# Gathering routed tokens with four 32-row matmul tiles in fp32, and normalising on GpSimd

## Chip, core and metric

One core of one Trainium2 chip. The time is the device time of one execution in microseconds, the median of the runs shown. Engines are called PE (TensorE matmul), PEld (its weight loads), DVE (VectorE), ACT (ScalarE), POOL (GpSimd) and SP (SyncE).

## What is computed

A gated cross-attention block and a mixture-of-experts block, one after another, on x of 16 batches of 128 tokens with 256 features, all in fp32:

```python
x = x + tanh(g_xattn[0]) * xattn(layernorm(x), ctx, ctx, Wq, Wk, Wv, Wo, bo)
x = x + tanh(g_ffn[0]) * ffn(layernorm(x), controller, f1, bias, f2)
```

The attention has 16 heads of 16 features and a causal mask. In the feed-forward block the tokens of a batch form 4 groups of 32. Each of 128 slots (32 experts x 4 sets) takes, in each group, the one token with the largest logit:

```python
grouped = x.reshape(B, g, t, d)                      # g groups of t = 32 tokens, d = 256
logits = einsum('bgtd,des->bgtes', grouped, controller) + tie
perm = (logits == max(logits, axis=-3, keepdims=True))
dispatched = einsum('bgtd,bgtes->bgesd', grouped, perm)
inner = relu(einsum('bgesd,desf->bgesf', dispatched, f1) + bias)
intermediate = einsum('bgesf,esfd->bgesd', inner, f2)
out = einsum('bgesd,bgtes->bgtd', intermediate, perm)
```

The change concerns `dispatched`, the gather of the tokens by a permutation matrix of zeros and ones.

## The kernel before

The kernel has one program for each engine, with its order written out by hand and semaphores between them. It has four stages: loads and the first statistics (to some 13 us), attention batch by batch (to some 198 us, each batch in four chunks `c` of four heads), **routing** (to 231.6 us), the experts (to 295 us), and the combination with the store of the result. The change touches routing and the last attention batch, which already does the routing's first steps.

Routing works on one batch of 128 tokens at a time. For batch `b`:

- DVE normalises the rows: `xn[:, b % 4]`, 128x256 (`normalize`, L843). For batches 0 to 3 this is done within the last attention batch, for the others four batches ahead, and DVE waits for `rl_ready` of the slot's former batch.
- ACT rounds the rows to fp32r, `rh` (`rows_high`, L676), and POOL subtracts, `rl = xn - rh` (`split_rows`, L285). The slot of `xn` has then been read, except for the transposes.
- PE transposes the rows (`transpose_r`, L379) into bank 0, ACT keeps them as `rT` (`keep_r`, L664), PE makes the logits in bank 1 (`logits`, L384).
- DVE adds the tie ramp (`add_ramp`, L885, tile `lt`), takes the maximum of each group (L890) and compares (L895), which gives the permutation `pc` (slot x token), in two buffers. POOL copies it to `permT` (`keep_perm`, L290), which the last stage reads again.
- PE transposes `pc` (`spread`, L392) into bank 2 or 7. DVE multiplies it by a mask of groups into `permb` (`spread`, L901): token x (group, slot), 128x512, where the rows of other groups are zero.
- PE gathers (L528): for each half `h` of the features and each part (`rh`, `rl`) one full matmul of 512 columns, accumulated over the parts. The result of each half fills one bank. There are two sets of two banks (`BD`), used in turn.
- ACT moves both banks to `routed` (`keep_d`, L670), 2 x 512 columns. For the last two batches DVE moves one of the halves (L1031).

PE's order in the iteration for batch `b` is: logits of `b+2`, transposes of the rows of `b+3`, transpose of the permutation of `b+1`, gather of `b`. DVE's is: ramp of `b+2`, normalisation of `b+4`, maximum and comparison of `b+2`, masked copy of `b+1`. In the first four iterations DVE also runs the 13 stages of the inverse roots (`rstd`) of the last four batches. ACT's is: round rows of `b+3`, keep `rT` of `b+3`, move the gather of `b`. The first four and last four iterations are written out, the rest are loops of four.

When all of `routed` is kept, DVE gathers the experts' inputs into `xe` (L1038), and the expert stage begins. Its matmuls L548, as L348, L352, L368 in attention and L611 at the end, use tiles of 32 columns of the array.

Of the kernel before, what the change touches and what calls it, by code (L numbers as in the profile page):

```python
# [25 lines left out]
P = 128  # L26
# [23 lines left out]
def build(nc, x, ctxT, wattn, gbo, ctrl, wexp, constf, out):  # L50
    with ExitStack() as ctx:
# [6 lines left out]
        bank = [ctx.enter_context(nc.psum_tensor(f"bank{i}", [P, 512], F32)) for i in range(8)]  # L58
# [45 lines left out]
        rh = sb("rh", [P, 4, E], F32R)  # L104
        rl = sb("rl", [P, 4, E], F32R)
        lt = sb("lt", [P, P])
        gmax = sb("gmax", [P, NG])
        pc = sb("pc", [P, 2, P])
        permT = sb("permT", [P, NB, P])
        permb = sb("permb", [P, 2, NG, P], F32R)  # L110
# [57 lines left out]
        rh_ready = sem("rh_ready")  # L168
        rl_ready = sem("rl_ready")
# [7 lines left out]
        pm_ready = sem("pm_ready")  # L177
# [10 lines left out]
        permT_kept = sem("permT_kept")  # L188
# [48 lines left out]
        def _(pool):  # L237
# [44 lines left out]
            def split_rows(b, k4):  # L282

                pool.wait_ge(rh_ready, b + 1)
                pool.tensor_tensor(rl[:, k4], xn[:, k4], rh[:, k4].bitcast(F32), ALU.subtract).then_inc(rl_ready, 1)  # L285

            def keep_perm(b, k):

                pool.wait_ge(perm_ready, b + 1)
                pool.tensor_copy(permT[:, b, :], pc[:, k, :]).then_inc(permT_kept, 1)  # L290

            for b in range(3):
                split_rows(b, b)
            with pool.Fori(0, NB // 4 - 1) as i:
                b = i * 4
                for k4 in range(4):

                    keep_perm(b + k4, k4 % 2)
                    split_rows(b + (k4 + 3), (k4 + 3) % 4)
            for k4 in range(4):  # L300
                keep_perm(NB - 4 + k4, k4 % 2)
                if k4 < 1:
                    split_rows(NB - 1, 3)

            pool.wait_ge(permT_kept, NB)
# [11 lines left out]
        def _(pe):  # L317
# [56 lines left out]
            BR, BL, BP = bank[0], bank[1], (bank[2], bank[7])  # L374
            BD = ((bank[5], bank[6]), (bank[3], bank[4]))
# [128 lines left out]
            def route(b, k4, early=False, left=NB):  # L504

                k = k4 % 2
                if left > 2:
# [3 lines left out]
                if left > 3:  # L512
                    pe.wait_ge(rn_ready, b + 4)
                    transpose_r((k4 + 3) % 4)
                if left > 1:
                    if early and b == 0:

                        pe.wait_ge(x1_ready, NB)
                    spread(b + 1, 1 - k, first=early and b == 0)
# [12 lines left out]
            for b in range(4):  # L532
                route(b, b, early=(b < 2))
            with pe.Fori(1, (NB - 4) // 4) as i:
                b = i * 4
                for k4 in range(4):
                    route(b + k4, k4)
            for k4 in range(4):
                route(NB - 4 + k4, k4, left=4 - k4)
# [37 lines left out]
            pe.wait_ge(d_kept_dve, 2)  # L577
# [51 lines left out]
        def _(act):  # L629
# [37 lines left out]
            def keep_d(b, k, halves=KH):  # L667
                act.wait_ge(d_done, b + 1)
                for h in range(halves):
                    last = act.activation(routed[:, h, bass.ds(b * NG, NG), :],  # L670
                                          bank[5 - 2 * k + h][:, :].rearrange("p (g s) -> p g s", g=NG), ACT.Copy)
                last.then_inc(d_kept, 1)

            def rows_high(b, k4):
                act.wait_ge(rn_ready, b + 1)
                act.activation(rh[:, k4], xn[:, k4], ACT.Copy).then_inc(rh_ready, 1)  # L676

            def softmax(b, k, loads=None, first=False, second=False, final=False):
                for c in range(NC):
# [27 lines left out]
                    if final and c >= 1:  # L707
                        if c >= 2:
                            act.wait_ge(rT_done, c - 1)
                            keep_r(6)  # L710
                        rows_high(c - 1, c - 1)
# [32 lines left out]
            def route(b, k4, left=NB):  # L744
                if left > 3:

                    rows_high(b + 3, (k4 + 3) % 4)
                    act.wait_ge(rT_done, b + 4)
                    keep_r()

                keep_d(b, k4 % 2, KH if left > 2 else 1)

            with act.Fori(0, NB // 4 - 1) as i:
                b = i * 4
                for k4 in range(4):
                    route(b + k4, k4)
            for k4 in range(4):
                route(NB - 4 + k4, k4, left=4 - k4)
# [22 lines left out]
        def _(dve):  # L781
            steps = [0]
# [5 lines left out]
            def rstd(stage, lo, hi):  # L788
# [10 lines left out]
                elif stage == 1:  # L799
                    dve.tensor_scalar(m, m, 0.5, None, ALU.mult)  # L800
                    dve.tensor_scalar(v, v, 1.0 / E, EPS, ALU.mult, ALU.add)
                    step(dve.tensor_tensor(q, q, q, ALU.mult))
                elif stage == 2:
                    step(dve.scalar_tensor_tensor(v, q, 0.25, v, ALU.mult, ALU.add))
                elif stage == 3:

                    dve.tensor_scalar(y.bitcast(I32), v.bitcast(I32), -0.5, RSQRT_SEED, ALU.mult, ALU.add)
                    step(dve.tensor_scalar(q, v, -0.5, None, ALU.mult))
                elif stage % 3 == 1:
                    step(dve.tensor_tensor(t, q, y, ALU.mult))  # L810
                elif stage % 3 == 2:
                    step(dve.tensor_tensor(t, t, y, ALU.mult))
                else:
                    step(dve.scalar_tensor_tensor(y, t, 1.5, y, ALU.add, ALU.mult))

            def rstd_ready():

                dve.wait_ge(dve_step, steps[0])

# [11 lines left out]
            rstd_ready()  # L831
# [55 lines left out]
            def pick(b, k, early):  # L887
# [4 lines left out]
                if not early:  # L892

                    dve.wait_ge(permT_kept, b - 1)
                dve.tensor_tensor(pc[:, k, :].rearrange("p (g t) -> p g t", g=NG), lg,  # L895
                                  gmax[:, :, None].to_broadcast([P, NG, T]), ALU.is_equal).then_inc(perm_ready, 1)
# [80 lines left out]
            def route(b, k4, early=False, left=NB, stages=()):  # L977

                for stage in stages[:2]:
                    rstd(stage, NB - 4, NB)  # L980
                if left > 2:
                    add_ramp(b + 2)
                if left > 4:

                    dve.wait_ge(rl_ready, b + 1)
                    normalize(b + 4, k4, rn_ready)
                for stage in stages[2:]:
                    rstd(stage, NB - 4, NB)
                if left > 2:
                    pick(b + 2, k4 % 2, early)  # L990
                if left > 1:
                    spread(b + 1, (k4 + 1) % 2)

# [15 lines left out]
            pick(0, 0, True)  # L1010
            finish_attention(NB - 2)
            add_ramp(1, 5)
            pick(1, 1, True)
# [4 lines left out]
            for b in range(4):  # L1018
                route(b, b, stages=range(4 * b, min(4 * b + 4, RSTD_STAGES)))
            rstd_ready()  # L1020
            with dve.Fori(1, (NB - 4) // 4) as i:
                b = i * 4
                for k4 in range(4):
                    route(b + k4, k4)
            for k4 in range(4):
                route(NB - 4 + k4, k4, left=4 - k4)

            for b in range(NB - 2, NB):

                dve.wait_ge(d_done, b + 1)  # L1030
                dve.tensor_copy(routed[:, 1, b * NG:(b + 1) * NG, :],  # L1031
                                bank[6 - 2 * (b % 2)][:, :].rearrange("p (g s) -> p g s", g=NG))\
                    .then_inc(d_kept_dve, 1)
# [26 lines left out]
            dve.wait_ge(d_kept_dve, 2)  # L1060
# [89 lines left out]
```

## Time and profile before

| | us |
|---|---|
| median of 3 runs | 329.9 |
| lowest, highest | 329.48, 330.55 |
| profiled execution, first to last instruction | 326.0 |

The span of the profiled execution is 3.9 us under the median of the runs: what lies before its first and after its last instruction is in the one and not in the other. Over the span PE is busy for 286.1 us, PEld 209.9, DVE 264.4, ACT 196.3 and POOL 112.3. Busy time is a sum over all stages. A stage that changes is read from the views of its own stretch: the table of stretches for how full each engine is, the groups of instructions for what one costs, the timeline for the distance from one batch to the next, and the chain for which of them set the end. A matmul in fp32 stands in the trace as two records, one in fp32r and a transpose as one. The duration of a record includes its way through the array, so matmuls that follow each other overlap: the distance of their starts is their cost.

### The profile page before, as it was taken

The page shows a single profiled execution, that of the slowest core. Times are in us where ns is not written, and L with a number is a line of the kernel's source. Part 1 is how long each engine was busy: PE and PEld are TensorE (multiplying, and loading weights), DVE is VectorE, ACT ScalarE, POOL GpSimd, SP SyncE. Part 2 cuts the span into 40 slices and gives each one's busy share as a digit, 9 for nine tenths or more (in the row PEclk, how much of TensorE's full clock was granted, in tenths as well). Part 3 has the DMA queues.
Part 4 walks back from the last instruction along what each step waited for, and adds up shares of the span by engine and source line. Part 5 has one row for each costly group of instructions (what it writes and reads, how often), then busy time and mean ns, then how long its engine had stood idle before and what let it go on. Part 6 is the DMA issues. An engine that isn't in the chain of part 4 may idle for free.

```text
span 326.0 us, 9319 instructions
## 1 busy us (share of the span) xinstructions
PE 286.1 (88%) x3088; PEld 209.9 (64%) x3088; DVE 264.4 (81%) x675; ACT 196.3 (60%) x738; POOL 112.3 (34%) x156
## 2 busy tenths in 40 slices
PE   2299899999999999999999968899687777787995
PEld 2247577777787778787877647677365444555662
DVE  1968988978787878787879868999899999985663
ACT  2057777777777777777777863687232233225663
POOL 4124554455445644563455561455000000000110
PEclk9999999999999999999999997999899999999999
DMA  7940000000000000000000000000045454300222
GB/s 208 369 182 4 18 18 0 19 18 17 0 16 16 16 0 16 16 16 0 16 0 0 2 2 0 1 2 0 0 131 135 151 136 129 97 2 16 80 80 82
DMA packets 12355, 16.41 MB, mean 50 GB/s; under 512 B 1200, under 2 KB 7728, under 8 KB 12336
## 3 DMA queue, kind: packets, MB, share of 16 engines
q1 hardware_dynamic: 11472, 14.83, 14.9%
q10 hardware_dynamic: 864, 1.33, 1.3%
q8 instruction: 11, 0.18, 0.3%
q14 instruction: 8, 0.07, 0.1%
HBM read 14.06 MB, written 2.10 MB: 50 GB/s over the span
## 4 chain that ended last, share of the span: by engine, by line
PE 57%; DVE 26%; issue 11%; DMA 2%; ACT 2%; POOL 1%; DVEq 0%; ACTq 0%; SPq 0%; POOLq 0%
PE bank L359 10%; PE bank L352 9%; PE bank L368 9%; DVE hb L1052 8%; PE bank L328 8%; PE bank L338 7%; PE bank L596 5%; PE bank L348 3%; PE bank L611 3%; DVE xe L1038 2%; DMA xs<-in_x_dram 2%; DVE nmax L912 2%; PE bank L528 1%; DVE permb L901 1%; DVE stats L824 1%
## 5 line engine op out<-in xcount | busy, mean ns | idle before, releaser
L688 ACT ACTIVATE pr<-bank,nmax 128x128 f32<-128x128 f32 x256 | 90.3, 368 | 25.1 <-PE bank L359 18.5
L263 POOL TENSOR_TENSOR pr<-pr,rsum 128x512 f32<-128x512 f32 x64 | 66.6, 1040 | 89.4 <-DVE rsum L861 89.1
L352 PE MATMUL bank<-kd,qz 128*32 128x128 f32 (+3 forms) x512 | 66.7, 437 | 0.0
L368 PE MATMUL bank<-pT,va 128*32 128x128 f32 x512 | 62.3, 274 | 1.7 <-ACT pT L653 1.3
L912 DVE TENSOR_REDUCE nmax<-bank 128x4 f32<-128x512 f32 x64 | 44.0, 687 | 19.9 <-PE bank L352 18.6
L688 ACT ACTIVATION_READ_ACCUMULATOR pr<-bank,nmax 128x1 f32 x256 | 52.9, 207 | 0.0
L368 PEld LDWEIGHTS bank<-pT,va 128*32 128x32 f32 x512 | 38.6, 110 | 17.1 <-ACT pT L653 2.5
L556 PE MATMUL bank<-hb,wx 128*128 128x256 f32 x128 | 37.5, 417 | 12.5 <-DVE hb L1052 12.5
L765 ACT ACTIVATE routed<-bank 128x512 f32 x32 | 19.1, 597 | 45.0 <-PE bank L556 45.0
L359 PE MATMUL bank<-cf,pr 128*128 128x128 f32 x256 | 42.0, 286 | 1.6 <-POOL pr L263 1.5
L1052 DVE TENSOR_SCALAR hb<-bank,wx 32x64 f32<-32x64 f32 x128 | 36.0, 281 | 2.9 <-PE bank L548 0.6
L359 PEld LDWEIGHTS bank<-cf,pr 128*128 128x128 f32 x256 | 26.8, 140 | 15.1 <-issue 11.5
L556 PEld LDWEIGHTS bank<-hb,wx 128*128 128x128 f32 x128 | 22.4, 195 | 19.6 <-DVE hb L1052 15.9
L313 POOL COPY pg<-permT 128x128 f32 x14 | 4.1, 294 | 87.5 <-PE bank L611 87.5
L653 ACT ACTIVATE pT<-bank 128x512 f32<-128x512 f32 x32 | 19.1, 598 | 18.0 <-PE bank L359 18.0
L328 PE MATMUL bank<-cT,w 128*128 128x128 f32 x128 | 18.1, 286 | 6.2 <-DMA w<-in_wattn_dram 5.6
L874 DVE COPY pT<-bank 128x512 f32<-128x512 f32 x32 | 22.1, 689 | 1.7
L843 DVE TENSOR_SCALAR xn<-xs,mv,rs 128x256 f32 (+1 forms) x32 | 23.4, 732 | 0.0
L1038 DVE COPY xe<-routed 128x512 f32 (+1 forms) x32 | 22.4, 710 | 1.0
L775 ACT ACTIVATE ys<-bank 128x512 f32<-128x512 f32 x32 | 17.3, 596 | 9.4 <-PE bank L596 9.4
L670 ACT ACTIVATE routed<-bank 128x512 f32 (+1 forms) x30 | 16.4, 595 | 8.9 <-PE bank L528 8.7
L848 DVE TENSOR_TENSOR kd<-bank,cf 128x512 f32<-128x512 f32 x32 | 21.4, 672 | 0.4 <-PE bank L328 0.4
(91 smaller groups left out, 538.8 us busy)
## 6 DMA issues: line engine op xcount, KB each, us to landing
wx<-in_wexp_dram SPq DMA_DIRECT2D x32, 256.5 KB, 2.7
cT<-in_ctxT_dram SPq DMA_DIRECT2D x16, 128.0 KB, 2.0
xs<-in_x_dram SPq DMA_DIRECT2D x4, 512.0 KB, 10.3
out_dram<-xs SPq DMA_DIRECT2D x16, 128.0 KB, 1.7
w<-in_wattn_dram ACTq DMA_DIRECT2D x4, 256.0 KB, 7.7
cf<-in_constf_dram ACTq DMA_DIRECT2D x1, 148.0 KB, 5.9
gb<-in_gbo_dram ACTq DMA_DIRECT2D x1, 129.0 KB, 7.6
ctrl_sb<-in_ctrl_dram SPq DMA_DIRECT2D x1, 128.0 KB, 10.7
```

What stands on the lines that cost most here:

```text
L263: pool.tensor_tensor(pr[:, c % 2], pr[:, c % 2], rsum[:, c * HC:(c + 1) * HC, None].to_broadcast([P, HC, P]), ALU.mult)\
L328: last = pe.matmul(dst[:, o * P:(o + 1) * P], weight[:, i, o * P:(o + 1) * P], src[:, i, :], start=(i == 0), stop=(i == KH - 1))
L338: last = pe.matmul(dst[:, 0:E], stationary, moving, start=(q == 0), stop=(q == len(parts) - 1))
L352: last = pe.matmul(bs[r, :, 0:(j + 1) * DP], qz[:, k, c // 2, c % 2, r], kd[:, k, c // 2, :, 0:(j + 1) * DP], start=False, stop=True, tile ...
L359: last = pe.transpose(BT[:, j * P:(j + 1) * P], pr[:, c % 2, j, :], ident)
L368: last = pe.matmul(BO[k][j * DP:(j + 1) * DP, o:o + P], va[:, k, c * HC + j, D * (1 - odd):][:, 0:DP], pT[:, c % 2, j * P:(j + 1) * P], st ...
L556: last = pe.matmul(BE[k][:, h * E:(h + 1) * E], wx[:, r, KH * P + h * P:KH * P + (h + 1) * P], hb[:, k].rearrange("p s g -> p (s g)"), sta ...
L688: last = act.activation(pr[:, c % 2, j, :], BS[c % 2][:, j * P:(j + 1) * P], ACT.Exp, bias=nmax[:, c * HC + j:c * HC + j + 1], accum_out=p ...
L843: dve.tensor_scalar(xn[:, k, :], xs[:, b, :], mv[:, b, 0:1], rs[:, bass.ds(b, 1)], ALU.subtract, ALU.mult).then_inc(ready, 1)
L912: dve.tensor_reduce(nmax[:, c * HC:(c + 1) * HC], BS[c % 2][:, :].rearrange("p (j t) -> p j t", j=HC), AX_X, ALU.max, negate=True).then_in ...
L1038: dve.tensor_copy(xe[:, k].rearrange("p h s g -> p h g s"), routed[:, :, :, bass.ds(e * NS, NS)]).then_inc(xe_ready, 1)
L1052: last = dve.tensor_scalar(hb[q, k, s, :], bank[k][q, 0:GROUPS], wx[q, r, KH * P + E:], 0.0, ALU.add, ALU.max)
```

## The change

1. The gather takes eight fp32 matmuls in place of four fp32r ones: for each half `h` and each group `g`, the 32 rows of the group in `xn` (as the stationary operand, 32x128) with the 32 rows of the permutation (128 columns), in the tile of the array at rows `32 g`. Each group writes its own bank (3 to 6), so the four banks hold one batch and there is one set, not two. `rh`, `rl`, `permb`, `rows_high` and `split_rows` are gone.
2. DVE copies the transposed permutation as it is into `pt` (128x128, two buffers).
3. The comparison writes `permT[:, b]` directly; `pc` and POOL's copy are gone.
4. ACT moves three of the four banks in one instruction of 768 elements, DVE the fourth (256 elements), after each batch.
5. POOL normalises batches 4 to 15. It waits for `d_done` of batch `b-4`, since the gather reads `xn` itself. DVE's last instruction of an inverse root counts `rs_ready`, for which POOL waits once.
6. The loops of routing are written out on all engines.

```diff
-        bank = [ctx.enter_context(nc.psum_tensor(f"bank{i}", [P, 512], F32)) for i in range(8)]
+        banks = ctx.enter_context(nc.psum_tensor("banks", [P, 8, 512], F32))
+        bank = [banks[:, i, :] for i in range(8)]
...
-        permb = sb("permb", [P, 2, NG, P], F32R)
+        pt = sb("pt", [P, 2, P])
...
+            def normalize(b):
+
+                pool.wait_ge(rn_ready, 4)
+                pool.wait_ge(rs_ready, 4 if b < NB - 4 else 5)
+                pool.wait_ge(d_done, b - 3)
+                pool.tensor_scalar(xn[:, b % 4, :], xs[:, b, :], mv[:, b, 0:1], rs[:, b:b + 1],
+                                   ALU.subtract, ALU.mult).then_inc(rn_ready, 1)
+
+            for b in range(4, NB):
+                normalize(b)
...
-            BR, BL, BP = bank[0], bank[1], (bank[2], bank[7])
-            BD = ((bank[5], bank[6]), (bank[3], bank[4]))
+            BR, BL, BP, BD = bank[0], bank[1], (bank[2], bank[7]), bank[3:7]
...
-                    pe.wait_ge(pm_ready, b - 1)
-                pe.transpose(BP[k][:, 0:P], pc[:, k, :], ident).then_inc(pm_done, 1)
+                    pe.wait_ge(pt_ready, b - 1)
+                pe.transpose(BP[k][:, 0:P], permT[:, b, :], ident).then_inc(pm_done, 1)
...
-                pe.wait_ge(pm_ready, b + 1)
-                pe.wait_ge(rl_ready, b + 1)
-                if not early:
-
-                    pe.wait_ge(d_kept, b - 1)
-                for h in range(KH):
-
-                    for q, part in enumerate((rh, rl)):
-                        last = pe.matmul(BD[k][h][:, :], part[:, k4, h * P:(h + 1) * P],
-                                         permb[:, k, :, :].rearrange("p g s -> p (g s)"), start=(q == 0), stop=(q == 1))
-                last.then_inc(d_done, 1)
...
+            def dispatch(b):
+
+                pe.wait_ge(pt_ready, b + 1)
+                if b >= 1:
+                    pe.wait_ge(d_kept, b)
+                    pe.wait_ge(d_kept_dve, b)
+                for h in range(KH):
+                    for g in range(NG):
+                        q = slice(g * T, (g + 1) * T)
+                        last = pe.matmul(BD[g][:, h * SLOTS:(h + 1) * SLOTS], xn[q, b % 4, h * P:(h + 1) * P],
+                                         pt[q, b % 2, :], start=True, stop=True, tile_position=(g * T, 0),
+                                         skip_group_check=True)
+                last.then_inc(d_done, 1)
+
+            for b in range(NB):
+                if b + 2 < NB:
                     pe.wait_ge(rT_ready, b + 3)
                     pe.wait_ge(lt_ready, b + 2)
                     logits()
...
+                if b + 3 < NB:
                     pe.wait_ge(rn_ready, b + 4)
...
+                    transpose_r((b + 3) % 4)
+                if b + 1 < NB:
...
+                    spread(b + 1, (b + 1) % 2, first=(b == 0))
+                dispatch(b)
...
+            def keep_d(b):
                 act.wait_ge(d_done, b + 1)
...
+                act.activation(routed[:, :, b * NG:(b + 1) * NG - 1, :],
+                               banks[:, 3:6, 0:KH * SLOTS].rearrange("p g (h s) -> p h g s", h=KH), ACT.Copy)\
+                    .then_inc(d_kept, 1)
...
-                dve.tensor_tensor(permb[:, k, :, :], bank[(2, 7)[k]][:, None, 0:P].to_broadcast([P, NG, P]),
-                                  groupmask[:, :, None].to_broadcast([P, NG, P]), ALU.mult).then_inc(pm_ready, 1)
+                if b >= 2:
+                    dve.wait_ge(d_done, b - 1)
+                dve.tensor_copy(pt[:, k, :], bank[(2, 7)[k]][:, 0:P]).then_inc(pt_ready, 1)
+
+            def keep_d(b):
+                dve.wait_ge(d_done, b + 1)
+                dve.tensor_copy(routed[:, :, (b + 1) * NG - 1, :],
+                                bank[6][:, 0:KH * SLOTS].rearrange("p (h s) -> p h s", h=KH)).then_inc(d_kept_dve, 1)
...
+            for b in range(NB):
+                stages = range(4 * b, min(4 * b + 4, RSTD_STAGES))
+                for stage in stages[:2]:
+                    rstd(stage, NB - 4, NB)
+                if b + 2 < NB:
+                    add_ramp(b + 2)
+                for stage in stages[2:3]:
+                    rstd(stage, NB - 4, NB)
+                if b + 2 < NB:
+                    pick(b + 2)
+                for stage in stages[3:]:
+                    rstd(stage, NB - 4, NB)
+                if b + 1 < NB:
+                    spread(b + 1, (b + 1) % 2)
+                keep_d(b)
```

## Rows read from the trace of the kernel before

**Rows 1.** The page: busy us, share of the span, instructions, by engine

```profile
PE 286.1 (88%) x3088; PEld 209.9 (64%) x3088; DVE 264.4 (81%) x675; ACT 196.3 (60%) x738; POOL 112.3 (34%) x156
```

**Rows 2.** Table of stretches: from:to, length, busy us per engine, PEclk, DMA

```profile
193.50:196.90 3.40, 1.57 (x17) 1.05 (x16) 2.85 (x7) 0.79 (x3) 1.42 (x4) 1.00 0.00 0
196.90:200.30 3.40, 3.40 (x15) 3.11 (x14) 2.58 (x15) 0.38 (x1) 0.00 (x0) 0.50 0.00 0
202.00:226.00 24.00, 22.03 (x123) 16.55 (x122) 22.21 (x63) 18.69 (x46) 11.89 (x23) 1.00 0.00 1
...
240.00:288.00 48.00, 37.65 (x508) 24.11 (x504) 45.35 (x124) 14.93 (x25) 0.00 (x0) 1.00 0.44 125
```

**Rows 3.** Groups of instructions: busy us, mean ns, idle before and releaser

```profile
L528 PE MATMUL bank<-permb,rh 128*128 128x512 f32 x32 | 14.7, 459 | 1.9 <-DVE permb L901 1.6
...
L901 DVE TENSOR_TENSOR permb<-bank,cf 128x512 fp32r<-128x512 f32 x16 | 10.8, 681 | 0.0
...
L670 ACT ACTIVATE routed<-bank 128x512 f32 (+1 forms) x30 | 16.4, 595 | 8.9 <-PE bank L528 8.7
...
L664 ACT ACTIVATE rT<-bank 128x256 f32<-128x256 f32 x16 | 6.2, 387 | 3.9 <-PE bank L379 3.8
...
L857 DVE COPY xT<-bank 128x256 f32<-128x256 f32 x16 | 6.7, 420 | 4.0 <-PE bank L321 4.0
...
L885 DVE TENSOR_TENSOR lt<-bank,cf 128x128 f32<-128x128 f32 x16 | 4.5, 282 | 1.2 <-PE bank L384 1.0 <-issue 0.3
```

**Rows 4.** Timeline, routing: start us, duration us, then what ended idle time before

```profile
198.65 0.78 PE L528 MATMUL bank<-permb,rh 128*128 128x512 f32 x1
...
208.70 0.50 PE L528 MATMUL bank<-permb,rh 128*128 128x512 f32 x1 [0.27 <-DVE permb L901]
...
220.44 0.25 PEld L379 LDWEIGHTS bank<-cf,xn 128*128 128x128 f32 x2
...
220.77 0.19 PEld L528 LDWEIGHTS bank<-permb,rh 128*128 128x128 f32 x1
...
221.10 0.41 DVE L843 TENSOR_SCALAR xn<-xs,mv,rs 128x256 f32 x1
...
222.03 0.52 PEld L384 LDWEIGHTS bank<-rT,ctrl_sb 128*128 128x128 f32 x4 [0.49 <-ACT rT L664]
...
225.12 0.50 PE L528 MATMUL bank<-permb,rh 128*128 128x512 f32 x1 [0.25 <-DVE permb L901]
```

**Rows 5.** Timeline, last attention batch: column tiles, then full-array transposes

```profile
189.16 0.43 PE L368 MATMUL bank<-pT,va 128*32 128x128 f32 x8 [0.35 <-DVE pT L874]
...
189.52 0.42 PEld L359 LDWEIGHTS bank<-cf,pr 128*128 128x128 f32 x4 [0.20 <-issue]
```

**Rows 6.** Groups of instructions on POOL, different shapes apart

```profile
L250 POOL TENSOR_TENSOR cTl<-cT,cTh 128x256 fp32r<-128x256 f32 x16 | 11.7, 729 | 0.3 <-ACT cTh L660 0.3
L255 POOL TENSOR_TENSOR xs<-xs,gb 128x256 f32 x14 | 8.9, 637 | 0.0
L313 POOL COPY pg<-permT 128x128 f32 x14 | 4.1, 294 | 87.5 <-PE bank L611 87.5
```

**Rows 7.** Timeline, last stage: tiled matmuls, and POOL that waits for them

```profile
302.02 0.40 PE L611 MATMUL bank<-ys,pg 128*32 128x256 f32 x4
...
302.62 0.29 POOL L313 COPY pg<-permT 128x128 f32 x1 [1.28 <-PE bank L611]
```

**Rows 8.** Timeline: end of batch 12's gather, and the first expert inputs

```profile
225.91 0.39 PE L528 MATMUL bank<-permb,rl 128*128 128x512 f32 x1
...
231.60 1.67 DVE L1038 COPY xe<-routed 128x512 f32<-128x512 f32 x3
```

**Rows 9.** The chain of waits at ACT, and timeline of POOL beside DVE

```profile
190.66 0.31 ACT rh L676
...
195.07 0.72 POOL L285 TENSOR_TENSOR rl<-xn,rh 128x256 fp32r<-128x256 f32 x1 [1.16 <-ACT rh L676]
...
195.41 0.53 DVE L895 TENSOR_TENSOR pc<-lt,gmax 128x128 f32<-128x128 f32 x1
```

More of the change, by code:

```diff
@@ L103, in build @@
         rT = sb("rT", [P, KH, P])
-        rh = sb("rh", [P, 4, E], F32R)
-        rl = sb("rl", [P, 4, E], F32R)
         lt = sb("lt", [P, P])
         gmax = sb("gmax", [P, NG])
-        pc = sb("pc", [P, 2, P])
         permT = sb("permT", [P, NB, P])
-        permb = sb("permb", [P, 2, NG, P], F32R)
+        pt = sb("pt", [P, 2, P])
         routed = sb("routed", [P, KH, GROUPS, SLOTS])
@@ L167, in build @@
         rn_ready = sem("rn_ready")
-        rh_ready = sem("rh_ready")
-        rl_ready = sem("rl_ready")
+        rs_ready = sem("rs_ready")
         rT_done = sem("rT_done")
@@ L176, in build @@
         pm_done = sem("pm_done")
-        pm_ready = sem("pm_ready")
+        pt_ready = sem("pt_ready")
         d_done = sem("d_done")
@@ L186, in build @@
         e_kept = sem("e_kept")
-        permT_kept = sem("permT_kept")
         yg_ready = sem("yg_ready")
@@ L280, in _ @@
             attend(NB - 1, 1, final=True)
[L282 to L305, printed above, removed]
+            def normalize(b):
[6 more added lines that the diff above has]
+                normalize(b)
+            pool.wait_ge(perm_ready, NB)
             for k in range(2):
@@ L502, in _ @@
             project_rows(BY, onTh, onTl, WO, y_done)
-            def route(b, k4, early=False, left=NB):
-                k = k4 % 2
-                if left > 2:
+            def dispatch(b):
[12 more added lines that the diff above has]
+                if b + 2 < NB:
                     pe.wait_ge(rT_ready, b + 3)
@@ L511, in route @@
                     logits()
-                if left > 3:
+                if b + 3 < NB:
                     pe.wait_ge(rn_ready, b + 4)
-                    transpose_r((k4 + 3) % 4)
-                if left > 1:
-                    if early and b == 0:
+                    transpose_r((b + 3) % 4)
+                if b + 1 < NB:
+                    if b == 0:
                         pe.wait_ge(x1_ready, NB)
-                    spread(b + 1, 1 - k, first=early and b == 0)
-                pe.wait_ge(pm_ready, b + 1)
-                pe.wait_ge(rl_ready, b + 1)
-                if not early:
-                    pe.wait_ge(d_kept, b - 1)
-                for h in range(KH):
-                    for q, part in enumerate((rh, rl)):
-                        last = pe.matmul(BD[k][h][:, :], part[:, k4, h * P:(h + 1) * P],
-                                         permb[:, k, :, :].rearrange("p g s -> p (g s)"), start=(q == 0), stop=(q == 1))
-                last.then_inc(d_done, 1)
[L532 to L539, printed above, removed]
+                    spread(b + 1, (b + 1) % 2, first=(b == 0))
+                dispatch(b)
             BH, BE = bank[0:2], bank[2:4]
@@ L576, in _ @@
             pe.wait_ge(d_kept, NB)
-            pe.wait_ge(d_kept_dve, 2)
+            pe.wait_ge(d_kept_dve, NB)
             pe.wait_ge(wx_loaded[0], 16)
@@ L665, in keep_r @@
                     .then_inc(rT_ready, 1)
-            def keep_d(b, k, halves=KH):
+            def keep_d(b):
                 act.wait_ge(d_done, b + 1)
[L669 to L676, printed above, removed]
+                act.activation(routed[:, :, b * NG:(b + 1) * NG - 1, :],
+                               banks[:, 3:6, 0:KH * SLOTS].rearrange("p g (h s) -> p h g s", h=KH), ACT.Copy)\
+                    .then_inc(d_kept, 1)
             def softmax(b, k, loads=None, first=False, second=False, final=False):
@@ L706, in softmax @@
                             keep_onT(1 - k)
[L707 to L711, printed above, removed]
+                    if final and c >= 2:
+                        act.wait_ge(rT_done, c - 1)
+                        keep_r(6)
             for k in range(2):
@@ L742, in _ @@
             keep_onT(1)
-            def route(b, k4, left=NB):
-                if left > 3:
-                    rows_high(b + 3, (k4 + 3) % 4)
+            for b in range(NB):
+                if b + 3 < NB:
                     act.wait_ge(rT_done, b + 4)
                     keep_r()
[L751 to L758, printed above, removed]
+                keep_d(b)
             with act.Fori(0, NE // 2) as i:
@@ L781, in _ @@
         def _(dve):
-            steps = [0]
+            steps, blocks = [0], [0]
             def step(ins):
@@ L812, in rstd @@
                     step(dve.tensor_tensor(t, t, y, ALU.mult))
-                else:
-                    step(dve.scalar_tensor_tensor(y, t, 1.5, y, ALU.add, ALU.mult))
+                elif stage < RSTD_STAGES - 1:
+                    step(dve.scalar_tensor_tensor(y, t, 1.5, y, ALU.add, ALU.mult))
+                else:
+                    blocks[0] += 1
+                    dve.scalar_tensor_tensor(y, t, 1.5, y, ALU.add, ALU.mult).then_inc(rs_ready, 1)
             def rstd_ready():
                 dve.wait_ge(dve_step, steps[0])
+                if blocks[0] > 0:
+                    dve.wait_ge(rs_ready, blocks[0])
             def statistics(lo, hi):
@@ L830, in _ @@
             statistics(0, XC)
-            rstd_ready()
+            dve.wait_ge(dve_step, steps[0])
             for stage in range(RSTD_STAGES):
@@ L885, in add_ramp, with pick @@
                 dve.tensor_tensor(lt[:, :], bank[of][:, 0:P], tie, ALU.add).then_inc(lt_ready, 1)
-            def pick(b, k, early):
+            def pick(b):
                 dve.wait_ge(lt_ready, b + 1)
@@ L891, in pick @@
                 dve.wait_ge(gmax_ready, b + 1)
-                if not early:
-                    dve.wait_ge(permT_kept, b - 1)
-                dve.tensor_tensor(pc[:, k, :].rearrange("p (g t) -> p g t", g=NG), lg,
+                dve.tensor_tensor(permT[:, b, :].rearrange("p (g t) -> p g t", g=NG), lg,
                                   gmax[:, :, None].to_broadcast([P, NG, T]), ALU.is_equal).then_inc(perm_ready, 1)
@@ L976, in _ @@
                     attend(b + k, k)
[L977 to L992, printed above, removed]
             dve.wait_ge(stats_ready, NB - 4)
@@ L1009, in _ @@
             add_ramp(0, 5)
-            pick(0, 0, True)
+            pick(0)
             finish_attention(NB - 2)
             add_ramp(1, 5)
-            pick(1, 1, True)
+            pick(1)
             low_part(NB - 1, 1)
@@ L1017, in _ @@
             dve.wait_ge(stats_ready, NB)
[L1018 to L1033, printed above, removed]
+            for b in range(NB):
+                stages = range(4 * b, min(4 * b + 4, RSTD_STAGES))
[11 more added lines that the diff above has]
+                    spread(b + 1, (b + 1) % 2)
+                keep_d(b)
             def stage(e, k):
@@ L1059, in _ @@
             dve.wait_ge(d_kept, NB)
-            dve.wait_ge(d_kept_dve, 2)
+            dve.wait_ge(d_kept_dve, NB)
             for e in range(XR - 1):
```

## Prediction

> **What bounds the kernel now.** I read the page first: over the whole span PE is busy for 88%, DVE for 81% [rows 1]. That is an average over stages, and the change touches one of them, the routing stage, from about 198 to 231.6 us, and the last attention batch ahead of it. So the view to read is the table of stretches. From 202 to 226 us PE is busy 22.0 of 24 us and DVE 22.2 of 24, ACT 18.7, POOL 11.9 [rows 2]: two engines are nearly full. The groups of instructions say with what. Per batch PE streams four 512-column matmuls, which follow each other every 0.23 us (0.93 us), DVE builds the masked copy (0.68 us) and normalises (0.41), and ACT takes 2 x 0.60 us to move the result [rows 3, 4]. One batch takes 2.05 us: the first gather matmul of batch 4 starts at 208.70 and that of batch 12 at 225.12, 16.42 us for eight [rows 4]. The waits name DVE's masked copy in front of some gathers, and ACT's rT in front of some logits (0.49 us at 222.03) [rows 4]: the loop is balanced, with no long wait anywhere. The first four batches are slower, 208.70 - 198.65 = 10.05 us, or 2.5 each, because DVE also runs the 13 stages of the last inverse roots there, and because the clock is at 0.50 of full (1.2 GHz) from 196.9 to 200.3 [rows 2, 4].
>
> **PE, part by part.** Removed: 4 x 0.23 = 0.93 us of streaming per batch. Added: eight fp32 matmuls, which stand as 16 records since each fp32 one is two, with 32 rows of contraction and 128 columns. No row of before shows tiles of 32 rows. 
>
> The Trainium skill (TensorEngine Tiling (Array Packing), section Tiling Modes) says that a change of tiling mode drains the array, and the 0.20 us row agrees. Its page TensorE: Matmul & The Clock Gate, section LDWEIGHTS, says that a 32x128 load takes as long as a 128x128 one; by that and loads one behind another the gather would be the serial 1.9 us, while the same page's part on packing has the tiles' loads overlap, which gives my 0.65. No row here decides between them.
>
> **DVE.** Per batch it loses 0.68 + 0.41 and gains a copy of 128 columns from PSUM (0.28 at most, by the addition of that size) and of 256 (0.42) [rows 3]: 1.93 us becomes 1.55 us. It has room then. **ACT** loses the rounding of the rows (0.42) and has one move of 768 elements in place of two of 512; from 0.39 us at 256 and 0.60 at 512 [rows 3] this is about 0.80. It has room too. **POOL** loses two short steps and gains the normalisation. No row has a one-input operation of 256 elements there. Below it stands the copy of 128 (0.29), above it the additions and subtractions of two inputs of 256 (0.64 and 0.73) [rows 6]. I take 0.55, just under two copies of 128, and keep 0.40 and 0.73 as ends.
>
> **What the change turns round.** Before, a slot of xn was free once its two rounded parts were made, long before its gather. Now the gather itself reads xn, and the same iteration that gathers b-3 must first transpose b. So POOL's normalisation of b waits for the gather of b-4, and on PE's queue the logits, which stand ahead, run meanwhile, but the transposes wait for POOL and the gather of b-3 is queued behind them. That is a closed loop: end of gather to POOL 0.20 (column-tiled matmuls end at 302.02 + 0.40, POOL starts at 302.62 [rows 7]), normalisation 0.55, POOL to PE 0.07, two row transposes and the perm transpose 0.33 [rows 4], the drain 0.20 [rows 5], the gather 0.65. Sum 2.00 us, against 2.05 us now. The 0.93 us that the gather loses are thus nearly all given back as waiting: PE would be idle for about 0.4 us in each batch.
>
> The other new condition, one set of gather banks in place of two, is hidden there: ACT's move ends 0.20 + 0.80 us after the gather, PE wants the banks back after 1.35 us. In the last three batches nothing is normalised any more, and this cover is gone: each then costs 0.20 + 0.80 + 0.06 + 0.65 = 1.7 us. From the end of the gather of batch 12 to the first xe: 3 x 1.7 + 0.20 + 0.80 + 0.1 = 6.2 us. Before, it was 231.60 - (225.91 + 0.39) = 5.3 us [rows 8]. That costs 0.9 us.
>
> **The stretch before.** In the last attention batch ACT's rounding of rows stands in the chain of waits for 0.31 us, and POOL's subtraction at 195.07 overlaps DVE's pc, which takes 0.53 there where 0.29 is usual [rows 9]. Both go: about -0.5 us. In batches 0 to 3 DVE is the bound, and it is relieved of 0.38 us each (1.5 in all); the loop of 2.00 us stands under it and the slow clock covers a part, so I count -1.0.
>
> **Sum**, against the profiled span of 326.0 us, which lies 3.9 us under the median of 329.9 (I keep that distance): -0.5 ahead, -1.0 in batches 0 to 3, 8 x (2.00 - 2.05) = -0.4 in batches 4 to 12, +0.9 in the tail: -1.0 us. 328.9 us.
>
> **Rivals.**
> 1. *POOL is quick* (0.40 us, or reaches PE sooner): the loop is 1.85 us, another 0.15 x 11 = 1.6 us less, 327.3. For it: POOL's copies cost little per element. Below about 1.8 us DVE and the chain over rT would bound. The Trainium skill (GPSIMD Engine Reference, section 3.1) has one-input bodies of up to two operations at 1.03 cycles per element, by which the normalisation, with the copy's fixed part, would be an estimated 0.4 us, this case.
> 2. *POOL is slow* (0.73 us or more), the case on the other side: the loop is 2.18 us, 12 batches hang on it, so +0.18 x 12 = +2.2 us over the sum, 331.1. It decides from a normalisation of some 0.73 us on, or 0.64 with POOL starting and releasing later than I think. For it: the two-input row is 0.73, and POOL's operations stretch beside DVE's with two inputs in SBUF.
> 3. *The row tiles run one after another*: the gather is 1.9 us, the loop 3.25, 16 x 1.2 = +19 us, 348. Against it: the column tiles of this kernel do run side by side.
> 4. *The clock falls in the routing stage*, since PE streams only some 1.2 of 2.0 us. Against it: from 240 to 288 us PE is busy 37.7 of 48 us at the full clock; for it: it fell after stretches with PE busy 1.6 of 3.4 us [rows 2]. The tail with its 0.65 us of gather in 1.7 is the likely place. Each 3.4 us at 1.2 GHz would cost about 1 us, 1 to 4 in all: 331.
> 5. *The change does not do what it says*, as the loop is not closed over POOL (it gets done within other waiting) and ACT, DVE and PE alone set the pace: 1.7 us a batch, 12 x 0.3 less, 325.5.
>
> **How the numbers follow.** The sum 0.42 (its own range 328.0 to 330.2), rival 1 0.20, rival 2 0.16, rival 3 0.07, rival 4 0.09, rival 5 0.06. Range: 326.8 to 332.4 takes in the sum, rivals 1, 2 and 4 for the most part and leaves 3 and 5 out. A change under 0.3% (1.0 us) is about what can't be told from none. The sum lies on that bound, so half of its cases count as faster: faster 0.21 + 0.20 + 0.06 = 0.47, same 0.19 + 0.05 (the near ends of rivals 2 and 4) = 0.24, slower 0.29.
>
> **What would show it.** In the profile after: 16 gather records within 0.65 us (1.9 would be rival 3); POOL's normalisation starting 0.2 us behind each gather and PE idle on POOL before the row transposes, in batches 4 to 15 (no such wait refutes the loop); a period of 2.00 us; the last three gathers each waiting for ACT's move, 1.7 us apart; no row rounding on ACT; the pc of the last attention batch at 0.29. I would be wrong by most if POOL's operation is far from 0.55 us, since every batch pays it in full.

## The result, and the profile after

The changed kernel takes 345.79 us (median of 4 runs, 343.93 to 346.27) against 329.69 us for the kernel before in the same comparison: a ratio of 1.0487, 95% interval 1.0444 to 1.0531. It is 16 us slower. The forecast was 328.9 us, with a range up to 332.4.

The spans of the two profiled executions are 344.0 and 326.0 us, 18 us apart. The span after lies 1.8 us under the time of its own run (345.76), and in the runs of the experiments below the distance is 1.7 to 2.3 us, for the kernel before too. So the 3.9 us between 326.0 and the median of 329.9 are not all time ahead of the first and behind the last instruction: the profiled execution of the kernel before was a quick one, of some 328 us, and about 2 of the 18 us are this difference between executions.

The page of the kernel after, its span, its busy times and the clock in 40 slices, which answer to [rows 1]:

```profile
span 344.0 us, 9534 instructions
...
PE 299.5 (87%) x3280; PEld 219.9 (64%) x3280; DVE 259.0 (75%) x677; ACT 189.8 (55%) x708; POOL 110.6 (32%) x136
...
PEclk9999999999999999999999885555559999999999
```

DVE, ACT and POOL have less work than before, in line with the change. PE has 13 us more, although its gather is shorter. The clock tells why: for six slices it is at half, and the matmul records in them are longer.

The table of stretches of the kernel after, around that (columns as in [rows 2]):

```profile
199.30:206.00 6.70, 4.45 (x54) 3.26 (x50) 5.39 (x26) 3.20 (x5) 3.34 (x3) 1.00 0.01 4
206.10:257.20 51.10, 43.44 (x353) 31.58 (x354) 25.57 (x77) 15.58 (x25) 11.74 (x12) 0.50 0.02 6
```

From 199.3 to 206 us PE is at 2.4 GHz but busy for only two thirds of the time. Then it is at 1.2 GHz for 51 us, until well into the expert stage. In this second stretch PE's busy share is 85%, which looks like a well-used engine. It isn't: at the low clock each record takes longer, and the busy share hides that PE still waits for POOL in each batch.

The timeline of the kernel after, one batch at the full clock (start, duration, what ended the idle time), with the POOL operation that the change added:

```profile
201.44 0.73 PE L496 MATMUL banks<-pt,xn 32*128 32x128 f32 x16
...
202.10 0.71 PE L367 MATMUL banks<-rT,ctrl_sb 128*128 128x128 f32 x4
...
202.40 1.22 POOL L283 TENSOR_SCALAR xn<-xs,mv,rs 128x256 f32<-128x256 f32 x1 [1.49 <-PE banks L496]
...
203.68 0.44 PE L362 MATMUL banks<-cf,xn 128*128 128x128 f32 x2 [0.87 <-POOL xn L283]
...
203.84 0.14 PEld L375 LDWEIGHTS banks<-cf,permT 128*128 128x128 f32 x1
...
204.15 0.54 PEld L496 LDWEIGHTS banks<-pt,xn 32*128 32x128 f32 x16 [0.17 <-issue]
```

This is the closed loop that the prediction described. The gather ends at 202.17, POOL starts 0.23 us later, works for 1.22 us to 203.62, and PE, which has long finished the logits, begins the loads of its transposes 0.05 us after that (the matmul records at 203.68), having idled 0.87 us. The last transpose's load ends at 203.98, and after a gap of 0.17 us the next gather begins. The gathers of batches 1 and 2 start at 201.44 and 204.15: 2.71 us for a batch, against 2.05 before [rows 4].

The waits between 204 and 240 us, the longest first in total (us, times, longest):

```profile
POOL xn L283 <- PE banks L496: 22.7, 10, 2.4
...
PEld banks L362 <- POOL xn L283: 6.9, 10, 1.1
```

PE and POOL wait for each other, ten times each, in every batch. Before, no wait of PE in routing came back in every batch: between 202 and 226 us it waited five times for `permb` and once for `pc`. And one batch at the low clock:

```profile
217.11 0.69 PE L362 MATMUL banks<-cf,xn 128*128 128x128 f32 x2 [0.35 <-POOL xn L283]
...
217.95 1.24 PE L496 MATMUL banks<-pt,xn 32*128 32x128 f32 x16
...
219.12 1.22 PE L367 MATMUL banks<-rT,ctrl_sb 128*128 128x128 f32 x4
```

The gather is 1.24 us in place of 0.73. From the start of the transposes to that of the gather it is 0.84 us in place of 0.48. Both are in the loop with POOL, so a batch takes 3.58 us (gathers at 214.37 and 217.95).

Where the 18 us of the span went, by the starts of the gathers: ahead of the first gather -0.4 (198.24 against 198.65), batches 0 to 4 +2.5 (12.55 against 10.05), batches 4 to 12 +12.2 (28.64 against 16.42), from there to the first xe +2.6 (248.52 - 239.43 = 9.1 against 231.60 - 225.12 = 6.5), and about +1.1 from there to the end, with the experts starting at the low clock.

### The profile page after: what moved, and what is told of

Same layout as the page of the kernel before. It is cut to its first block, busy times and chain, and to the rows that moved or that the text cites. A ratio compares the mean times of both kernels' runs of the same rounds, so it can differ in the third digit from the quotient of the medians.

```text
span 344.0 us, 9534 instructions
## 1 busy us (share of the span) xinstructions
PE 299.5 (87%) x3280; PEld 219.9 (64%) x3280; DVE 259.0 (75%) x677; ACT 189.8 (55%) x708; POOL 110.6 (32%) x136
## 4 chain that ended last, share of the span: by engine, by line
PE 63%; DVE 18%; issue 9%; POOL 5%; DMA 2%; ACT 2%; ACTq 0%; DVEq 0%; POOLq 0%; SPq 0%
PE banks L343 9%; PE banks L336 9%; PE banks L352 8%; PE banks L312 8%; DVE hb L999 8%; PE banks L322 7%; PE banks L496 5%; PE banks L571 4%; POOL xn L283 4%; PE banks L332 3%; PE banks L586 3%; PE banks L362 2%; DVE xe L985 2%; DMA xs<-in_x_dram 2%; PE banks L531 2%
## 5 line engine op out<-in xcount | busy, mean ns | idle before, releaser
L658 ACT ACTIVATE pr<-banks,nmax 128x128 f32<-128x128 f32 x256 | 90.5, 369 | 24.8 <-PE banks L343 18.7
L336 PE MATMUL banks<-kd,qz 128*32 128x128 f32 (+3 forms) x512 | 66.0, 433 | 0.0
L352 PE MATMUL banks<-pT,va 128*32 128x128 f32 x512 | 62.3, 274 | 1.4 <-ACT pT L628 1.0
L878 DVE TENSOR_REDUCE nmax<-banks 128x4 f32<-128x512 f32 x64 | 44.0, 687 | 19.2 <-PE banks L336 17.9
L658 ACT ACTIVATION_READ_ACCUMULATOR pr<-banks,nmax 128x1 f32 x256 | 53.1, 207 | 0.0
L352 PEld LDWEIGHTS banks<-pT,va 128*32 128x32 f32 x512 | 38.6, 110 | 16.8 <-ACT pT L628 2.2
L531 PE MATMUL banks<-hb,wx 128*128 128x256 f32 x128 | 38.3, 424 | 12.2 <-DVE hb L999 12.1
L343 PE MATMUL banks<-cf,pr 128*128 128x128 f32 x256 | 42.0, 286 | 1.6 <-POOL pr L259 1.5
L999 DVE TENSOR_SCALAR hb<-banks,wx 32x64 f32<-32x64 f32 x128 | 36.0, 281 | 3.7 <-PE banks L523 1.3
L343 PEld LDWEIGHTS banks<-cf,pr 128*128 128x128 f32 x256 | 26.8, 140 | 15.2 <-issue 11.3
```

The lines of the kernel that those rows point to most:

```text
L336: last = pe.matmul(bs[r, :, 0:(j + 1) * DP], qz[:, k, c // 2, c % 2, r], kd[:, k, c // 2, :, 0:(j + 1) * DP], start=False, stop=True, tile ...
L343: last = pe.transpose(BT[:, j * P:(j + 1) * P], pr[:, c % 2, j, :], ident)
L352: last = pe.matmul(BO[k][j * DP:(j + 1) * DP, o:o + P], va[:, k, c * HC + j, D * (1 - odd):][:, 0:DP], pT[:, c % 2, j * P:(j + 1) * P], st ...
L531: last = pe.matmul(BE[k][:, h * E:(h + 1) * E], wx[:, r, KH * P + h * P:KH * P + (h + 1) * P], hb[:, k].rearrange("p s g -> p (s g)"), sta ...
L658: last = act.activation(pr[:, c % 2, j, :], BS[c % 2][:, j * P:(j + 1) * P], ACT.Exp, bias=nmax[:, c * HC + j:c * HC + j + 1], accum_out=p ...
L878: dve.tensor_reduce(nmax[:, c * HC:(c + 1) * HC], BS[c % 2][:, :].rearrange("p (j t) -> p j t", j=HC), AX_X, ALU.max, negate=True).then_in ...
```

## Experiments

Two things changed at once, a long POOL operation in a closed loop and the clock. The theory: the loop is the cause, and PE's idle time in it brings the clock down. The rivals: the 32-row gather leaves PE so little to stream that the clock falls in any case, or POOL's operation harms wherever it stands. Four kernels (the next four) were run beside the kernel before, which took 329.05 us there, and three more later, beside one of 329.25.

### More slots: the same POOL operation, out of the loop

```diff
-        xn = sb("xn", [P, 4, E])
+        xn = sb("xn", [P, 8, E])
...
-                pool.wait_ge(d_done, b - 3)
-                pool.tensor_scalar(xn[:, b % 4, :], ...
+                if b >= 8:
+                    pool.wait_ge(d_done, b - 7)
+                pool.tensor_scalar(xn[:, b % 8, :], ...
```

(Gather and transposes read slot `b % 8` accordingly.)

> The changed kernel with eight slots of xn in place of four; POOL's normalisation then waits for the gather of eight batches before and runs ahead. If the closed loop over POOL is the cause and the low clock only follows from PE's waiting in it, the clock stays up and a batch takes about 1.75 us (ACT's move and the gather: 0.14 + 0.81 + 0.05 + 0.73), so some 326 to 328 us. If the clock falls whatever POOL does, since the gather leaves PE too little to stream, a batch takes some 2.3 to 2.6 us at 1.2 GHz and the time is 334 to 338 us. If POOL's 1.22 us slows the others by itself, in or out of the loop, the period stays above 2.7 us and the time near 345 us.

Measured: 323.71 us, ratio to before 0.9837 (0.9815 to 0.9858). The gathers start 1.69 us apart from batch 3 to batch 15. POOL does the same 1.22 us per batch, and the clock stays at 2.4 GHz until the last gather. The table of stretches of this kernel:

```profile
204.00:224.00 20.00, 18.89 (x265) 14.87 (x263) 16.03 (x59) 13.22 (x23) 7.50 (x8) 1.00 0.01 2
```

So neither POOL's operation outside the loop nor the 32-row gather makes the kernel slower or brings the clock down in routing: the loop does. The kernel was quicker than the 326 to 328 us expected, with 1.69 us for a batch in place of 1.75. The clock does fall in the last gather and stays low from about 225 to 235.5 us, into the experts. The kernel with filled waits below has such a stretch too.

### The operation on DVE, in the loop

```diff
+                if b == 7:
+                    rstd_ready()
+                if b + 4 < NB:
+                    dve.wait_ge(d_done, b + 1)
+                    normalize(b + 4, b % 4, rn_ready)
                 keep_d(b)
```

(POOL's `normalize` is taken out.)

> The changed kernel with DVE normalising batches 4 to 15 right behind the gather that frees the slot; four slots as in the change. The loop stays closed but has 0.41 us in it in place of 0.23 + 1.22. If the length of POOL's operation is the term that was wrong, a batch takes 0.1 + 0.41 + 0.05 + 0.33 + 0.2 + 0.73 = 1.85 us at the full clock: about 328 us. If the low clock has its own cause, about 2.75 us a batch and 339 us.

Measured: 325.07 us, ratio 0.9889 (0.9848 to 0.9930), a batch at 1.74 us. Four slots and a closed loop, but with 0.41 us in it. Expected were 1.85 us and 328 us. The timeline of this kernel shows the loop whole:

```profile
213.58 0.71 PE L356 MATMUL banks<-rT,ctrl_sb 128*128 128x128 f32 x4
...
213.72 0.41 DVE L795 TENSOR_SCALAR xn<-xs,mv,rs 128x256 f32<-128x256 f32 x1
...
214.19 0.44 PE L351 MATMUL banks<-cf,xn 128*128 128x128 f32 x2
```

The gather ended at 213.66, DVE is done at 214.13, and PE transposes at 214.19, when the logits have only just gone in. The loop is still there and still sets the pace (0.06 + 0.41 + 0.06 + 0.31 + 0.17 + 0.73 = 1.74 us), but that is no more than 0.05 us a batch over the kernels without it. What made it dear was the length of the operation in it.

### Both undone: eight slots and DVE

> Eight slots and DVE normalising, where the kernel before did: the gather of the change with the normalisation of before. No loop and no long POOL operation. If the 32-row gather is itself no loss, a batch takes 1.75 to 1.95 us (DVE has 1.95 us of work) and the time is 326 to 328.5 us; if the 32-row gather takes the clock down by itself, 334 us or more.

```diff
+                if b == 4:
+                    rstd_ready()
+                if b + 4 < NB:
+                    if b >= 4:
+                        dve.wait_ge(d_done, b - 3)
+                    normalize(b + 4, (b + 4) % 8, rn_ready)
```

(POOL's `normalize` is taken out and `xn` has eight slots.)

Measured: 325.21 us, ratio 0.9857 (0.9820 to 0.9895), 1.69 us a batch from batch 3 on. The period is that of POOL and eight slots. The two medians are 1.5 us apart, but the runs of each kernel overlap (323.09 to 325.69 against 323.34 to 324.54), and the profiled execution here has one stretch more at the low clock in the last stage (near 293 to 296 us), so nothing is read from that. It is the rest of the change alone: the 32-row gather, the unmasked copy, the permutation kept once and the other parts together bring about 1.4%. How it divides among them was not tested.

### PE kept busy while it waits

```diff
+                    if b >= 1:
+                        for q in range(5):
+                            pe.matmul(BR[:, E:2 * E], wh[:, 0, 0, 0:P], wh[:, 0, q % KH, :], start=True, stop=True)
                     pe.wait_ge(rn_ready, b + 4)
```

> The changed kernel with five matmuls of 256 columns more per batch (from batch 1), made of weights into an unused half of a bank, ahead of PE's wait for POOL; their result is used by nothing. They fill PE's wait of 0.87 us and nothing else. If the clock's fall comes from PE's idle time, it stays up: a batch takes 2.7 us, set by POOL in the loop, and the time is 334 to 336 us. If the clock falls all the same, a batch takes 4 us or more and the time is 350 us or more.

Measured: 335.63 us, ratio 1.0204 (1.0185 to 1.0223). The gathers start 2.71 or 2.72 us apart from batch 1 to batch 12, and the table of stretches of this kernel has the full clock over the whole of it:

```profile
204.00:231.00 27.00, 24.23 (x282) 19.33 (x280) 16.21 (x53) 11.95 (x20) 12.23 (x10) 1.00 0.01 2
```

Work that nobody needs makes the changed kernel 10.2 us faster. This splits the loss: the low clock in routing costs about 345.8 - 335.6 = 10.2 us (10.3 by the spans, 344.0 - 333.7; the two kernels stand in different comparisons, with the kernel before at 329.69 and 329.05), and the loop at the full clock 335.6 - 323.7 = 11.9 us against the same kernel with more slots. The low clock in routing follows from PE's idle time in the loop, since nothing else was altered here. Two low stretches are left and don't touch this: both kernels have one from 195.8 to 199.2 us, ahead of the loop, and this one has another from its last gather on, from about 236.9 to 247 us, as the kernel with eight slots has.

### How many slots it takes

The loop of 2.71 us is closed over one batch. With one slot more it is closed over two.

> The changed kernel with one slot of xn more, five in place of four. If the closed loop is one batch long, a fifth slot makes it two batches long: gather to POOL 0.14 to 0.23, normalisation 1.22, release 0.05, transposes 0.33, drain 0.2, gather 0.73, in all 2.7 us spread over two batches, so it lies under the 1.69 us that ACT's move and the gather take, and the time is that of eight slots, 323 to 325 us, with a batch at 1.69 us. If POOL has to be many batches ahead, the period stays above 2 us and the time above 329 us.

```diff
-        xn = sb("xn", [P, 4, E])
+        xn = sb("xn", [P, 5, E])
...
-                pool.wait_ge(d_done, b - 3)
+                if b >= 5:
+                    pool.wait_ge(d_done, b - 4)
```

Measured: 323.45 us (323.20 to 323.63) against 329.25 us, ratio 0.9837 (0.9800 to 0.9874), and 1.69 us a batch. A kilobyte more per partition turns a loss of 5% into a gain of 1.6%. Gather and transposes read slot `b % 5`. This is the quickest of the kernels tried, with that of eight slots. What bounds it now, in its timeline:

```profile
213.34 0.81 ACT L645 ACTIVATE routed<-banks 128x768 f32<-128x768 f32 x1 [0.47 <-PE banks L497]
213.51 1.22 POOL L284 TENSOR_SCALAR xn<-xs,mv,rs 128x256 f32<-128x256 f32 x1 [0.47 <-PE banks L497]
...
213.88 0.14 PEld L376 LDWEIGHTS banks<-cf,permT 128*128 128x128 f32 x1
...
214.22 0.57 PEld L497 LDWEIGHTS banks<-pt,xn 32*128 32x128 f32 x16 [0.20 <-issue]
214.25 0.73 PE L497 MATMUL banks<-pt,xn 32*128 32x128 f32 x16
...
215.04 0.81 ACT L645 ACTIVATE routed<-banks 128x768 f32<-128x768 f32 x1 [0.47 <-PE banks L497]
```

ACT's move ends at 214.15, the gather's loads start at 214.22, the gather ends at 214.98 and ACT starts again at 215.04: 0.81 + 0.07 + 0.76 + 0.06 = 1.70 us. It is the one set of banks. That is read from the timeline; no kernel with a second set was run. PE alone would be hardly quicker: the load for the transpose of the permutation ends at 214.02, and with the gap of 0.17 us that stands there in the change the gather's loads would start at 214.19. POOL waits 0.47 us in each batch and is in nobody's way.

### What POOL's operation costs

POOL normalises the left 128 columns and DVE the right ones, with four slots.

```diff
-                pool.tensor_scalar(xn[:, b % 4, :], xs[:, b, :], mv[:, b, 0:1], rs[:, b:b + 1],
+                pool.tensor_scalar(xn[:, b % 4, 0:P], xs[:, b, 0:P], mv[:, b, 0:1], rs[:, b:b + 1],
...
+                    dve.wait_ge(d_done, b + 1)
+                    dve.tensor_scalar(xn[:, b % 4, P:E], xs[:, b + 4, P:E], mv[:, b + 4, 0:1], rs[:, b + 4:b + 5],
+                                      ALU.subtract, ALU.mult).then_inc(rn_right, 1)
```

> The change with four slots, POOL normalising the left 128 columns of each batch and DVE the right 128. If POOL's operation costs by the element (1.22 us for 256, with some 0.2 fixed), it is 0.7 us and the loop is 2.2 us at the full clock, the time 329 to 331 us; if its cost is mostly fixed (1.0 us or more), the loop is 2.5 us and the time 334 us, or 340 us and more if the clock falls with it.

Measured: 332.37 us, ratio 1.0110 (1.0061 to 1.0158), 2.34 us a batch, and the clock stays up in the loop (1.00 from 200.3 to 231 us). The groups of instructions, of this kernel and then of the kernel after:

```profile
L284 POOL TENSOR_SCALAR xn<-xs,mv,rs 128x128 f32<-128x128 f32 x12 | 10.1, 845 | 24.0 <-PE banks L497 24.0
```

```profile
L283 POOL TENSOR_SCALAR xn<-xs,mv,rs 128x256 f32<-128x256 f32 x12 | 14.7, 1222 | 32.7 <-PE banks L496 32.7
```

Half the columns take 0.85 us, all of them 1.22. If the cost is a fixed part and one per column, the two points give (1.22 - 0.85) / 128 = 2.9 ns per column and 0.47 us that doesn't depend on them. DVE isn't what makes the operation long: it takes 1.22 us in the change, where DVE is busy for 3.49 of 8 us (208 to 216 us), and 1.22 with five slots, where DVE is busy for 6.61 of the same 8. Neither expectation was met: it is neither mostly by the element nor mostly fixed. The loop got shorter by 2.71 - 2.34 = 0.37 us, the operation's own difference, which shows once more that the loop pays it in full.

### The order of the tiles

With eight slots, both halves of one tile, then the next tile, in place of the four tiles in turn.

```diff
-                for h in range(KH):
-                    for g in range(NG):
+                for g in range(NG):
+                    for h in range(KH):
```

> Eight slots, and the gather's matmuls in another order: both halves of the features of one tile of the array, then the next tile, in place of the four tiles in turn. If tiles run side by side only where neighbours in the queue lie on different tiles, the four records of one tile follow each other (3 x 0.11 before the next tile can start): the gather takes about 1.3 to 1.6 us in place of 0.73, the period 2.3 to 2.5 us and the time 334 to 338 us. If the order doesn't matter, 1.69 us and 324 us.

Measured: 325.25 us, ratio 0.9893 (0.9843 to 0.9943), 1.73 us a batch. The gather in the timeline of this kernel, and under it that of eight slots in the first order:

```profile
211.24 0.75 PE L497 MATMUL banks<-pt,xn 32*128 32x128 f32 x16
```

```profile
207.81 0.73 PE L497 MATMUL banks<-pt,xn 32*128 32x128 f32 x16
```

0.75 us in place of 0.73. The first of my two expectations, 1.3 to 1.6 us, did not come true: neighbours in the queue needn't lie on different tiles, and the tiles run side by side all the same. The time is 1.5 us over that of eight slots. 0.04 us a batch explains 0.6 of it, and this profiled execution, like that of eight slots with DVE, has a low stretch in the last stage.

## Why the prediction was wrong

**What held.** The loop is as described, link by link, and so is what stands in front of it. At the full clock a batch takes 2.71 us. The predicted sum was 0.20 + 0.55 + 0.07 + 0.33 + 0.20 + 0.65 = 2.00; measured it is 0.23 + 1.22 + 0.05 + 0.31 + 0.17 + 0.73. The gather was forecast at 0.65 and takes 0.73, side by side: rival 3 is refuted. ACT's move was forecast at 0.80 from [rows 3] and takes 0.81. The last batches, where nothing is normalised, were to be 1.7 us apart, and are 1.69 to 1.70 in the kernel with filled waits (2.53, 2.22 and 2.20 at the low clock in the change). The pc of the last attention batch is 0.29 us again, rows are no longer rounded on ACT, and the first gather came 0.4 us earlier where 0.5 was forecast. That the loop of banks is hidden was right for the change, and by the timeline it is what bounds the kernels with more slots, at 1.69 us. There the loop over POOL isn't the limit, and 323.5 to 325.2 us stand near rival 5's 325.5.

**The step that failed first: the price of POOL's normalisation.** I took 0.55 us, and 0.73 as the upper end. It is 1.22 us, 0.67 more, in each of the twelve batches. The upper end came from the additions and subtractions of two inputs [rows 6], on the argument that one input can't cost more than two. That was an argument and no bound: the operation has two arithmetic steps and two scalars for each partition, and no row of the trace had such an operation on POOL. The result is that one input cost more than two: 1.22 us against 0.64 and 0.73 for as many columns. This term alone puts the loop at 2.7 us, and 12 batches of it at +8 us, 337 us, out of the range. The kernel with filled waits, which has just this, took 335.6 us. Rival 2 was the right mechanism, with its place and its sign; only its price, and so its time of 331, was short.

The estimate of 0.4 us fell with it. By the Trainium skill (GPSIMD Engine Reference, section 3.1) a one-input body of up to two operations runs at 1.03 cycles per element, which made that estimate. The trace disagrees: 1.22 us for 256 elements per partition, and 2.9 ns for each by the two sizes measured.

**The second: the clock.** Rival 4 named the fall of the clock and priced it at 1 to 4 us, counting on short low stretches as the one in [rows 2]. In the changed kernel it lasted 51 us and cost 10.2 by the kernel with filled waits. I had treated the two rivals as separate. They are one chain: the longer operation made PE idle, the idle PE was given 1.2 GHz, and the lower clock lengthened the parts of the loop that are on PE, 0.87 us a batch (3.58 - 2.71). Ahead of the fall PE was busy for 4.45 of 6.70 us (199.3 to 206.0). With the waits filled it was busy for 6.12 of the same 6.70, and the clock stayed. Rival 4 was priced at the forecast's period of 2.00 us, of which 1.2 are streamed. At the period of rival 2 taken to its end, 2.7 us, the same 1.2 us leave PE nothing to stream for 1.5, and that case was not asked for.

**The tail.** +0.9 us was forecast from the end of batch 12's gather to the first xe. It is 248.52 - 240.67 = 7.85 us against 5.3, so +2.6, at the low clock. With five slots and the full clock it goes as forecast: three gathers 1.69 us apart, and 226.04 - 220.06 = 5.98 us where 6.2 was the sum.

**The sum**, 0.4 us of gain ahead, losses of 2.5, 12.2, 2.6 and 1.1 us, stands against the forecast -0.5, -1.0, -0.4, +0.9 and nothing. The 3.9 us that I added to the span were some 2 us too many, as said under the result; that would have lowered the forecast, and isn't what failed. The range was too narrow because a term that twelve batches pay in full was given an end from operations of another kind.

## What to carry to other kernels

When a step moves to another engine and reads or writes a buffer of few slots, follow the slot round once: who frees it, who fills it, who waits behind that. If the loop closes within one iteration, every link in it is on the critical path, however idle its engine looks; one slot more was the whole remedy here. An operation that no row shows on its new engine has no upper bound from its neighbours there: let the range reach to where it would hurt, and then price the clock at the period that this gives.

## What the runs showed of the hardware

- GpSimd's tensor_scalar with two scalars per partition took 1.22 us for 128x256 fp32 and 0.85 us for 128x128, where DVE takes 0.41 and 0.35 us.
- Four fp32 tiles of 32 rows run side by side: 16 records of 128 columns in 0.73 us, in turn or tile by tile (0.75). Each load of 32x128 is 0.185 us long, one of 128x128 0.190 (L368) and one of 128x32 0.110 (L353; all from the groups of the kernel with five slots), but the sixteen loads stand within 0.57 us, so they overlap. Two statements of the Trainium skill (TensorE: Matmul & The Clock Gate, section LDWEIGHTS and Part 3 on packing) were set against each other in the prediction. Both hold here: the length of a load goes by its columns, and loads of different row tiles overlap.
- PE's clock stayed at 1.2 GHz for 51 us while the records had PE busy 85% of the time. In the same program with five useless matmuls of 256 columns per batch it was at 2.4 GHz from 199.3 us into the last gather, which starts at 236.38.
